# Output projection in three products of rounded parts, one chain of roots for two norms, and a reordered mixing stage (one Trainium2 core)

## What is computed

```python
mod = (silu(c) @ wmod).reshape(4, 6, 1, 256); sa, ca, ga, sb, cb, gb = ...   # |ga|, |gb| at least 0.25
h = layernorm(x) * (1 + ca) + sa
xn = rms_scale * h / (norm(h) / 16 + 1e-8) * split_scale
K = sigmoid(xn @ W_K); u, g_in, g_out = split(xn @ W_ugg, 3)
u = u * sigmoid(g_in) * (1 - K)
outputs[t] = K[t-1] * outputs[t-1] + u[t]
x = x + ga * ((outputs * sigmoid(g_out)) @ W_out + h)
h = layernorm(x) * (1 + cb) + sb
x = x + gb * moe(h)      # softmax gate, top 2 of 8 experts, h @ W1 -> gelu -> @ W2
```

## Time and profile before

| | us |
|---|---|
| median of 3 runs (lowest to highest) | 717.42 (715.46 to 718.61) |
| profiled execution, its own time | 716.57 |
| its span in the trace | 714.5 |
| PE busy | 676.1 |
| DVE busy | 505.8 |
| ACT busy | 415.6 |
| POOL busy | 397.9 |

### The profile page before, as it was taken

One profiled execution on the slowest core, in us unless ns is written; L12 is line 12 of the kernel. 1 busy time (PEld: TensorE's weight loads), 2 busy tenths in 40 slices (PEclk: granted clock), 3 DMA queues, 4 the chain that ended last, 5 costly groups with the idle time before them and its releaser, 6 DMA issues.

```text
span 714.5 us, 16030 instructions
## 1 busy us (share of the span) xinstructions
PE 676.1 (95%) x4794; PEld 618.5 (87%) x4794; DVE 505.8 (71%) x1750; ACT 415.6 (58%) x1067; POOL 397.9 (56%) x316
## 2 busy tenths in 40 slices
PE   5799999999999999889999999999999999999993
PEld 2578888788888888889899999999999999999993
DVE  4978789999889888576755566557875575475552
ACT  4555665556564655475556666656666566475561
POOL 2065545877768476276773546347666355373533
PEclk9799999999999999999999999999999999999998
DMA  8280111302012421346553454566654655644433
GB/s 302 89 278 0 60 61 45 121 23 98 32 61 73 136 91 62 91 83 171 106 112 62 82 123 74 131 146 168 166 97 73 152 106 113 148 73 70 72 51 43
DMA packets 50219, 72.24 MB, mean 101 GB/s; under 512 B 5904, under 2 KB 42076, under 8 KB 50144
## 3 DMA queue, kind: packets, MB, share of 16 engines
q0 software_dynamic: 16384, 27.02, 21.5%
q1 hardware_dynamic: 33760, 44.32, 20.2%
HBM read 48.32 MB, written 23.01 MB: 100 GB/s over the span
## 4 chain that ended last, share of the span: by engine, by line
PE 75%; DVE 9%; DMA 5%; issue 5%; ACT 3%; POOL 2%; SPq 0%; DVEq 0%; POOLq 0%; ACTq 0%
PE yb L1172 22%; PE mm L1036 19%; PE mm L1145 16%; PE yb L1061 6%; PE yb L1145 2%; DMA out_x<-ysb,tokb 2%; PE tp L1145 2%; PE tp L1136 2%; DMA gbr<-mod_rows,xm 1%; PE tp L1051 1%; DMA h2all<-in_L_wmod 1%; PE mm L1152 1%; DVE hl L1622 1%; ACT xnb L802 1%; DVE ytmp L1643 1%
## 5 line engine op out<-in xcount | busy, mean ns | idle before, releaser
L700 POOL DMA_INDIRECT out_x<-ysb,tokb x68 | 110.8, 1630 | 166.5 <-DVE ysb L1651 117.0
L958 ACT ACTIVATE hh<-mm,vT 128x256 fp32r<-128x256 f32 (+1 forms) x222 | 105.4, 475 | 134.8 <-PE mm L1145 108.7
L1172 PE MATMUL yb<-SH,hh 128*128 128x256 f32 x528 | 152.8, 289 | 4.5 <-DVE hl L1622 3.0
L1172 PE MATMUL yb<-SH,hl 128*128 128x256 f32 x528 | 147.3, 279 | 0.4 <-issue 0.4
L1172 PE MATMUL yb<-SL,hh 128*128 128x256 f32 x528 | 147.3, 279 | 0.4 <-issue 0.4
L1622 DVE TENSOR_TENSOR hl<-mm,hh 128x256 fp32r<-128x256 f32 (+1 forms) x222 | 89.1, 406 | 68.6 <-ACT mm L959 51.9
L1145 PE MATMUL mm<-fh,SH 128*128 128x256 f32 x396 | 111.9, 282 | 2.7 <-issue 1.5
L1145 PE MATMUL mm<-fl,SH 128*128 128x256 f32 x396 | 110.9, 280 | 1.3 <-issue 1.3
L1145 PE MATMUL mm<-fh,SL 128*128 128x256 f32 x396 | 110.4, 279 | 0.0
L1036 PE MATMUL mm<-xh,WH 128*128 128x512 f32 x256 | 107.5, 420 | 1.6 <-DVE xl L1378 1.4
L1172 PEld LDWEIGHTS yb<-SH,hh 128*128 128x128 f32 x528 | 99.6, 189 | 6.2 <-DVE hl L1622 4.6
(11 more groups left out here) (273 smaller groups left out, 1480.7 us busy)
## 6 DMA issues: line engine op xcount, KB each, us to landing
xin<-disp_x SPq DMA_DIRECT2D x72, 132.0 KB
wraw<-in_L_ffn_W SPq DMA_DIRECT2D x8, 1024.0 KB
h2all<-in_L_ffn_W SPq DMA_DIRECT2D x8, 1024.0 KB
xb<-in_L_attn_x SPq DMA_DIRECT2D x8, 512.0 KB, 6.9
out_x<-x2b SPq DMA_DIRECT2D x8, 512.0 KB
mb<-mod_rows SPq DMA_DIRECT2D x3, 768.0 KB, 6.2
wraw<-in_L_attn_W_ugg SPq DMA_DIRECT2D x1, 1536.0 KB, 11.9
gbr<-mod_rows,xm POOLq DMA_INDIRECT x72
```

Of the source, the lines that this page charges most:

```text
L700: e.indirect_dma_start(out=out_rows, out_offset=bass.IndirectOffsetOnAxis(ap=tokb[:, j:j + 1], axis=0), in_=ysb[:, j, :], in_offset=None, ...
L958: e.activation(hh[:, f, c_], u, ACT.Gelu_apprx_tanh, bias=bias)
L1172: i = e.matmul(yb[0][:, j * D:(j + 1) * D], a[:, f, j * 128:(j + 1) * 128], b[:, f, :], start=(f == 0 and j == 0 and t == 0), stop=(f == N ...
```

## The change

1. `project` makes three products of rounded parts (ogh*woh, ogh*wol, ogl*woh) for each of its four token tiles: 12 F32R matmuls in place of 4 float32 ones.
2. For that, each block gets an ACT instruction `o_round` (ob into ogh) and a DVE instruction `o_remainder` (ogl = ob - ogh); the output gate is multiplied in place in ob. ob stays single, so the remainder stands ahead of the next block's recur in DVE's queue. Each batch gets `wout_round` on ACT and `wout_remainder` on DVE. `wog` is one buffer.
3. LayerNorm 1's root of group g+2 and the norm's root of group g+1 are one chain on tensors twice as wide (`ln1`), of 9 instructions for the root instead of 11; the same shorter root serves LayerNorm 2. The chain moves from ahead of recur(g,0) to behind add_y(g-1), beside top2; only the four statistics instructions (`ln1_sums`) stay.
4. kb has 2 blocks instead of 4, with the carried column in `ck`, one small ACT copy per block of the even groups. On ACT ln2_square(g-1) moves ahead of gates 1, ln1_scale(g+2) behind them.

```diff
             def gate_wout(b):
-                past(e, "projected", 8 * (b - 1))
-                e.tensor_tensor(wog[b % 2][:, :, :], wo[:, :, :], bc(mod(b, 2), 4), ALU.mult)\
+                past(e, "wout_low", b)
+                e.tensor_tensor(wog[:, :, :], wo[:, :, :], bc(mod(b, 2), 4), ALU.mult)\
                     .then_inc(S["wout_gated"], 1)
...
             def gates_in(g, hc):
                 n = 4 * g + hc
-                past(e, "scanned", n - 3)
-                past(e, "k_ready", n - 3)
-                link(e, e.activation(kb[:, hc, 0:1], kb[:, hc, T:T + 1] if g % 2 else zcol[:, :], ACT.Copy), "act_own")
+                past(e, "scanned", n - 1)
+                past(e, "k_ready", n - 1)
+                link(e, e.activation(kb[:, n % 2, 0:1], ck[:, hc:hc + 1] if g % 2 else zcol[:, :], ACT.Copy), "act_own")
...
+            def o_round(g, hc):
+                n = 4 * g + hc
+                e.wait_ge(S["o_gated"], n + 1)
+                past(e, "projected", n - 1)
+                e.activation(ogh[:, n % 2, :], ob[:, :], ACT.Copy).then_inc(S["o_high"], 1)
+
+            def wout_round(b):
+                e.wait_ge(S["wout_gated"], b + 1)
+                past(e, "projected", 8 * b)
+                e.activation(woh[:, :, :], wog[:, :, :], ACT.Copy).then_inc(S["wout_high"], 1)
...
+                if g % 2 == 0:
+                    wout_round(g // 2)
...
                 if g == 0:
                     ln1_scale(1)
-                elif g + 2 < NG:
-                    ln1_scale(g + 2)
+                elif g < NG - 1:
+                    ln2_square(g - 1)
+                o_round(g, 0)
                 gates_in(g, 1)
                 gate_out(g, 1)
...
+                if 0 < g < NG - 2:
+                    ln1_scale(g + 2)
+                if 0 < g < NG - 1:
                     ln1_xn(g + 1)
...
+                o_round(g, 1)
                 gates_in(g, 2)
...
                 gates_in(g, 3)
+                o_round(g, 2)
...
             def project(g, hc):
                 n = 4 * g + hc
-                e.wait_ge(S["o_gated"], n + 1)
-                e.wait_ge(S["wout_gated"], g // 2 + 1)
+                e.wait_ge(S["o_low"], n + 1)
+                e.wait_ge(S["wout_low"], g // 2 + 1)
...
                 for j in range(4):
-                    i = e.matmul(yb[j // 2][:, (j % 2) * D:(j % 2 + 1) * D], og[:, n % 2, j * 128:(j + 1) * 128],
-                                 wog[(g // 2) % 2][:, hc, :], start=(hc == 0 and j % 2 == 0), stop=(hc == 3),
-                                 skip_group_check=True)
+                    for t, (a, b) in enumerate(((ogh, woh), (ogh, wol), (ogl, woh))):
+                        i = e.matmul(yb[j // 2][:, (j % 2) * D:(j % 2 + 1) * D], a[:, n % 2, j * 128:(j + 1) * 128],
+                                     b[:, hc, :], start=(hc == 0 and j % 2 == 0 and t == 0), stop=(hc == 3 and t == 2),
+                                     skip_group_check=True)
...
+            def o_remainder(g, hc):
+                n = 4 * g + hc
+                e.wait_ge(S["o_high"], n + 1)
+                e.tensor_tensor(ogl[:, n % 2, :], ob[:, :], ogh[:, n % 2, :].bitcast(F32), ALU.subtract)\
+                    .then_inc(S["o_low"], 1)
...
                 recur(g, 0)
                 if g >= 1:
                     add_y(g - 1)
-                if g >= 2:
-                    weave(top2(g - 2))
+                if g % 2 == 0:
+                    wout_remainder(g // 2)
+                o_remainder(g, 0)
+                roots = ln1(g + 2 if g < NG - 2 else None, g + 1) if 0 < g < NG - 1 else iter(())
+                some(8, roots)
+                weave(roots, *([top2(g - 2)] if g >= 2 else []))
                 recur(g, 1)
...
+                    chains = [ln2_stats(g - 1)] + ([place(g - 2), gate_weights(g - 2)] if g >= 2 else [])
+                    some(4, *chains)
+                    o_remainder(g, 1)
+                    weave(*chains)
...
                 recur(g, 2)
+                o_remainder(g, 2)
```

More of the change, by code:

```diff
@@ L966, in act_program @@
             h2t_copy_half(g - 1, 0)
+            o_round(g, 3)
             for i in range(NE):
@@ new lines, in ln1_sums, with ln1 @@
+            def ln1_sums(g):
+                e.wait_ge(S[X_LOADED[g % 3]], 16 * (g // 3 + 1))
+                for j in range(4):
+                    i = e.bn_stats(bst[:, 0, j, :], xb[g % 3][:, j, :])
+                i.then_inc(S["x_summed"], 1)
+            def ln1(stats, norm):
+                y2 = rsn[:, (stats if norm is None else norm + 1) % 2, :, :]
+                at_ = slice(0 if stats is not None else 1, 2 if norm is not None else 1)
+                d = nt[:, 6, :]
+                if stats is not None:
+                    e.wait_ge(S["x_summed"], stats + 1)
+                    for j in range(4):
+                        i = e.bn_aggr(mv[:, 0, j, :], bst[:, 0, j, :])
+                    yield from lk(e, i, "dve_a")
+                if norm is not None:
+                    e.wait_ge(S["h_squared"], norm + 1)
+                    i = e.tensor_scalar(nt[:, 1, :], ss[:, norm % 2, :], 1.0 / D, 1e-34, ALU.mult, ALU.max)
+                    if stats is None:
+                        yield from lk(e, i, "dve_a")
+                if stats is not None:
+                    yield from lk(e, e.tensor_scalar(nt[:, 0, :], mv[:, 0, :, 1], 1e-5, None, ALU.add), "dve_a")
+                    past(e, "x_scaled", stats - 1)
+                yield from rsqrt(nt[:, at_, :], y2[:, at_, :], nt[:, 4 + at_.start:4 + at_.stop, :])
+                if stats is not None:
+                    e.scalar_tensor_tensor(rsb[:, stats % 2, :], mv[:, 0, :, 0], -1.0, y2[:, 0, :], ALU.mult, ALU.mult)\
+                        .then_inc(S["x_stats"], 1)
+                if norm is not None:
+                    yield from lk(e, e.tensor_tensor(d, nt[:, 1, :], y2[:, 1, :], ALU.mult), "dve_a")
+                    yield from lk(e, e.tensor_scalar(d, d, 1e-8, None, ALU.add), "dve_a")
+                    past(e, "xn_ready", norm - 1)
+                    e.reciprocal(rin[:, norm % 2, :], d).then_inc(S["rms_ready"], 1)
@@ L1561, in tile_counts @@
                 yield
-            weave(ln1_stats(0))
+            ln1_sums(0)
+            weave(ln1(0, None))
             e.wait_ge(S["mod_made"], 1)
@@ L1573, in dve_program @@
             weights_low(0, 1)
[L1574 removed]
+            weave(ln1(None, 0))
             weights_low(1, 0)
@@ L1588, in dve_program @@
                     e.wait_ge(S["hx_ready"], NG - 1)
-                    for q in range(4):
+                    split_low(e, 0, 0)
+                    o_remainder(g - 1, 3)
+                    for q in range(1, 4):
                         split_low(e, 0, q)
@@ L1611, in dve_program @@
                 recur(g, 3)
+            o_remainder(NG - 1, 3)
             a, b, c_ = (wsl[:, q, :, :] for q in range(3))
```

108 lines of the change are left out of this document (51 added, 57 removed).

## The result

The changed kernel takes 759.12 us (median of 4 runs, 754.54 to 763.28); the kernel before, on the same chip, 718.01 (715.46 to 726.64). The two medians lie 41 us apart, a ratio of 1.0573; the ratio on record is 1.0526, with a 95% interval from 1.0475 to 1.0578, which is 38 us. Slower by either. The profiled execution took 758.89 us with a span of 756.8, 42.3 more than the 714.5 of before. The forecast was 756.

The account below looks back on a forecast made before the run. The mixing stage was taken as bound by PE, with DVE close behind at single points. The terms -10.2 + 35 + 9 + 5.6 + 1.5 - 1.4 gave +39.5 on 716.6, so 756 us, range 728 to 778.

Parts of the forecast that it names:

- the layout: Group 5 of the mixing stage timed, queues in new order, zero at project(4,3): 6.0 us of stalls.
- group 1: Mixing stage, the group without top2: forecast to stay near zero added delay.
- groups 2 to 6: Full mixing groups: stalls of 7 us each, 35 in all, plus 9 for late project(g,0) in groups 2, 4 and 6.
- The products: project on PE: 12 F32R matmuls take 1.41 us instead of 1.73, saving 10.2 us over 32 projects.
- The start: Group 0: project(0,0) at 43.8 instead of 39.5, 4.3 us late, and 1.3 more at project(0,2).
- Rank's stall: Group 5: PE reaches rank at 9.2, the top-2 choice is ready at 12.9, a stall of 3.7 us.
- The stall of 1.8 at project(g,1): Group 5: PE wants project(5,1) at 18.8, its remainder on DVE ends at 20.6, a stall of 1.8 us.
- The clock rival: Nine stalls of 3 to 4 us could each bring 2 us of lower clock: +16, 772 us; chance 0.18.
- project(g,0): Groups 2, 4 and 6: W_out's rounding and remainder stand ahead of the block's own, about 3 us late each, 9 together.
- The end: project(7,3), in the first expert tile, waits for a rounding and a remainder: 1.5 us.
- POOL's hold: DVE's remainders wait up to 2.4 us for POOL's product: 756 us, chance 0.45; without it 16 less, 740, chance 0.17.
- PE keeps its gain: Rival: PE stays the bound of the mixing stage and keeps the 10.2 us: 706 us; chance 0.11.

Follow-up runs that it names:

- e1: Kernel before with project as 12 F32R matmuls per block instead of 4 float32 ones, no rounding or remainder instructions: 713.86 us against 720.98, ratio 0.9898.
- e5: Changed kernel with the remainder made by a one-input tensor_reduce that copies ob, instead of ob - ogh: 750.16 us, ratio 1.0393 to the kernel before.
- e10: Kernel before with project as 4 F32R matmuls per block (one product) instead of 4 float32 ones: 699.30 us against 704.91, ratio 0.9919.
- e2: Changed kernel with o_round(g,0) ahead of ln2_square(g-1) on ACT instead of behind it: 750.08 us, ratio 1.0402 to the kernel before.

## Why the prediction was right, and where not

The forecast of 756 stands against 758.89 for the profiled execution. The sign and the mechanism were those of the layout: DVE waits for a rounding that stands behind ln2_square, POOL holds the remainders, and PE waits for the choice and for ogl. The closeness of the sum is in part luck. By its own steps, as delays of project(g,3) after less before (the first matmul of each on PE's timeline):

| | forecast | measured |
|---|---|---|
| group 0 (start +5.6, four products -1.3) | +4.3 | +4.05 |
| group 1 (near zero, -1.3) | -1.3 | +2.23 |
| groups 2 to 6 (35 + 9 - 1.4 - 6.4) | +36.2 | +30.99 |
| group 7 (1.5 - 1.3) | +0.2 | +3.96 |
| expert tiles | 0 | +1.07 |
| sum | +39.4 | +42.30 |

Groups 2 to 6 came out 5.2 us under, groups 1 and 7 together 7.3 over; the errors cancel.

- *The products*: 1.41 us per project, as said. As a term of the sum it is sound only while nothing else becomes late: e1, with nothing added, kept 7 of the 10 us by the medians and 4.9 in the stage.
- *The start*: project(0,0) at 42.52, not 43.8. The DMA for ga began at 29.48 here and at 30.72 before, and wog at 33.92 for 35.16; against that it is 4.2 late, as forecast (4.3).
- *Rank's stall*: 3.7 forecast for group 5, 3.15 measured; DVE's wait in front of ogl 2.7 forecast, 2.67 measured; the wait in front of the gate weights 1.9 and 1.85. Rank's figure hides two errors. Counted from project(4,3) at 216.29, the layout ended the mean at 3.9 and it ended at 6.1, because POOL's product held it for 2.27 us. The layout let POOL hold the remainders but gave the mean 0.1 us, though the row of 2.09 was in hand. The remainder was done at 9.5 instead of 7.3, project(5,0) waited 1.61 us that the layout had not, PE stood at rank at 11.2 instead of 9.2, and the choice was made at 14.3 instead of 12.9.
- *The stall of 1.8 at project(g,1)*: it doesn't show as a wait of PE in group 5. The matmuls behind rank ran slowly instead (7.18 us for 24 where the layout had 5.5). But project(5,1) started at 238.07, 0.06 us behind the end of its ogl (237.33 + 0.68), as it does in groups 3, 4 and 6 too: the remainder still set its start, and the slow matmuls filled the time until then. Group 5 of e5 shows the same step without the low clock. Rank stalls there for 3.18 us, the clock stays at 1.00 (first row, columns as in the earlier trace rows), and project(5,1) waits 1.43 us:

```profile
223.90:227.90 4.00, 4.00 (x22) 3.17 (x23) 3.54 (x8) 1.86 (x5) 2.40 (x1) 1.00 0.00 0
```

```profile
223.88 0.19 PE L1149 MATMUL tp<-selb,upper 128*128 128x32 bf16 x1 [3.18 <-DVE selb L1500]
...
231.26 0.38 PE L1091 MATMUL yb<-woh,ogh 128*128 128x256 f32 x1 [1.43 <-DVE ogl L1395]
```

From rank to project(5,1) it is 7.38 us there at the full clock, and 7.39 (238.07 - 230.68) in the changed kernel at the lower. From project(g,0) to project(g,1) the changed kernel takes 6.0, 7.8, 5.4, 5.1 and 4.9 us in groups 2 to 6 over the 7.06 of an undisturbed group (7.38 before, less 0.32), 29 in all, of which rank's stalls are 17.4. I had 5.7 each, so 28.5. The clock rival was thus half true. Its mechanism happened in these groups, its +16 on top did not: in group 5, by these two figures, the lower clock cost nothing, since it ran in time that would else have been waited away; the same start right behind ogl says so of groups 3, 4 and 6.

- *project(g,0)*: 3 us in the even groups was too much; it waited 1.4 to 1.6 us in groups 3 to 6 alike, in the odd ones too, where I had nothing (in group 5 by the late mean, above). That is why the full groups came out even (6.1, 6.3, 6.7, 5.8, 6.2 us) where I had 5.7 and 8.7 in turn.
- *Group 1* I left at zero because it has no top2. But its rounding also stands behind ln2_square: project(1,0) waited 1.82 us for ogl and mm2 1.46 for the scan.
- *The end*: 1.5 was too small. recur(7,3) started late, behind two SL remainders of the expert tile that took 3.48 us together, and its rounding and remainder followed; project(7,3) waited 2.76 us.
- *POOL's hold*: 16 us forecast between the two layouts, 10 measured in the stage (e5), with a longest of 2.80 us where I had up to 2.4 over 0.7.

The rival "PE keeps its gain" fell with the result, and e1 shows where it would have held: with nothing added to DVE and ACT, rank waits 2 us in the whole stage and 7 of the 10 us remain. So the gain is lost to the rounding and the remainder, not to the products.

## What to carry to other kernels

Splitting an operand into a rounded part and a remainder is paid less in their busy time (here 0.63 us on ACT and 0.68 on DVE per block; the 32 remainders by themselves were worth 7 us of 41) than in the two hand-overs between in-order queues: ask what stands ahead of the rounding on one engine, and what stands behind the remainder on the other. An engine that has 1.4 us to spare at one point can be the next bound, whatever its busy share; test it by shortening the bounding engine's work alone, as e10 did. Moving work to another place in a full queue mostly moves the wait to another consumer. A slow stretch behind a stall costs only what no later wait would have taken anyway: look how long the next operand has been ready when the slow stretch ends.

## What the runs showed of the hardware

- In the changed kernel each of the five stalls of PE at rank, 2.83 to 5.00 us long in otherwise dense work, came with the lower clock: the 4 us behind them ran at 0.50 to 0.57, those in group 3 are in the next row. I had taken such stalls to be too short. It is not so each time: in e5 the 4 us behind a stall of 3.18 us (group 5), and in e10 those behind one of 3.22 us (at 163 us), ran at 1.00. So the length of a stall alone doesn't tell.

```profile
154.00:158.00 4.00, 3.81 (x14) 3.04 (x15) 3.75 (x9) 1.78 (x5) 3.01 (x2) 0.50 0.54 206
```

- A 512-column DVE subtraction with two SBUF inputs took up to 2.80 us beside POOL's product (2.88 in e2), a tensor_reduce of the same size with one input never over 0.69 (e5). The mean of four elements, a tensor_scalar with one input, took 2.27 us beside POOL's product and 0.17 without one.
- One product instead of three gained no more than three did (5.6 us against 7.1, each against before). Only these two, which leave the low parts out (e1, e10), were faster than before, by about 1%; no version tried that makes the whole product was.
